# Tree feed-forward: leaves gathered by row from a DRAM table, dotted on VectorE and summed by TensorE through diagonals

## Chip, cores and metric

One core of one Trainium2 chip runs the whole program. The time is device microseconds from start to end of the program on that core; lower is better.

## What is computed

Eight layers follow one another on x, which is 8 x 256 tokens of width 256: each takes a layer norm of x and adds its result to x. The change lies in the second layer, a feed-forward network of 8 binary trees with 255 nodes each:

```python
logits = x @ W_in.T + b_in                      # x is the normed input, W_in is 2040 x 256
decisions = (logits > 0).reshape(B, 8, 255)
acts = silu(logits).reshape(B, 8, 255)
current = 0; dmap = one_hot(current, 255)
for d in range(7):                              # walk from the root to a leaf
    moves = decisions at node current
    current = (current - (2**d - 1)) * 2 + moves + (2**(d + 1) - 1)
    dmap = dmap + one_hot(current, 255)
out = (acts * dmap).reshape(B, 2040) @ W_out.T  # only the 8 nodes on each path count
```

A tree has 127 inner nodes and 128 leaves, and a token ends in exactly one leaf of each tree. The first layer is a cross attention without a softmax, and the third (a masked cross attention with 16 heads) starts when the second has been added to x.

## The kernel before

The five engines have one instruction stream each, written out by hand, with semaphores between them; nothing is planned by a compiler. x stays in SBUF as 16 tiles of 128 tokens. A pair (`i` from 0 to 3) is four such tiles, 512 tokens. Their normed rows `xln` are transposed to `xT` (`transpose_rows` on TensorE, `evacuate_xT` on ScalarE).

The tree stage is a loop over 4 pairs and within each over 8 trees `p`. One turn of it is called a step here. In each step TensorE computes logits with the nodes on the partitions and the tokens along the row: 127 inner nodes (c = 0) and 128 leaves (c = 1), each of two matmuls over the halves of the 256 inputs (L1665). VectorE compares the inner logits with the bias and writes `dec0` (L757). ScalarE computes silu of both banks into `act0` (L1342). One step later TensorE multiplies the decisions with the ancestor matrix `anc` (L1674): for each node the number of right turns minus left turns to it, and where this equals `tgt`, the node is on the token's path. VectorE writes `msk0`, act where it is equal and zero elsewhere (L749). Two steps later TensorE multiplies `msk0` with the output weights `woutT`, for four token tiles and both halves of the nodes (L1687), and sums all 8 trees in PSUM banks 0 and 1. At the end of a pair VectorE adds them to x (`residual`, L666), and the last pair's addition releases the mask load of the third layer (L480).

VectorE also does work of later stages in the stage: layer norm statistics of the next pair (p = 2, followed by `rstd_of` on GpSimd), its rows (p = 3), low bits of weight slices for a later layer (`low_bits`: a mask L670 and a reduction L672 over 1024 each, six slices a pair), sums and ternary rounding of the weights `stage_w1` and `stage_w2` (L698, L712 to L716). SyncE loads the six slices `seen` of the next pair when `Ff.low` says that the last ones were read. ScalarE's queue issues five DRAM to DRAM copies of later weights (L1331) right before the stage, 11 MB in all.

The fp32 matmuls stand in the trace as two records each. GpSimd issues indirect DMAs only in the last layer (`send` L616, the output rows L632).

## Time and profile before

| | |
|---|---|
| median of 3 runs | 1639.69 us (1639.01 to 1641.97) |
| profiled execution, its own time | 1637.88 us |
| its span, first to last instruction | 1636.2 us |
| TensorE busy | 1437.3 us, 88% |
| VectorE busy | 1073.6 us, 66% |
| ScalarE busy | 755.9 us, 46% |
| GpSimd busy | 116.6 us, 7% |
| tree stage, from the page's slices and the chain | 71.5 to 311.2 us |

Busy times of engines overlap, so they don't add up to the span. Engines in the rows: PE is TensorE's matmuls, PEld its weight loads, DVE VectorE, ACT ScalarE, POOL GpSimd, SP SyncE; a q behind a name is the engine's sequencer. A row of the trace gives the start in us, the duration in us, the engine, the line of the program, the operation, what it writes and reads, and in brackets how long the engine sat idle before it and what released it. Of several operations in one row (x8) the duration is that of the group.

### The profile page before, as it was taken

The numbers are of one execution on the slowest core, as the hardware profiler recorded it, in microseconds if no ns is written. First come the engines' busy times: TensorE is split into PE (matmuls) and PEld (weight loads), VectorE is DVE, ScalarE is ACT, GpSimd is POOL, SyncE is SP. The second block draws the span as 40 slices with busy tenths as digits, with TensorE's granted clock in tenths as the row PEclk, the third lists the DMA queues.
The fourth block names the chain that finished last, engine by engine and source line by source line (L and its number), as shares of the span: only waits on it lengthen the run. The fifth ranks groups of instructions, "written<-read, shape, count | busy, mean of one in ns | idle before, by whom it ended". The sixth has DMA issues, their size and how long they took to land.

```text
span 1636.2 us, 26350 instructions
## 1 busy us (share of the span) xinstructions
PE 1437.3 (88%) x9842; PEld 1075.0 (66%) x9849; DVE 1073.6 (66%) x2358; ACT 755.9 (46%) x1264; POOL 116.6 (7%) x168
## 2 busy tenths in 40 slices
PE   7999999878887995799888999999997889999557
PEld 5666666557783443477786878787773677788446
DVE  4455675778877874688856464555548988886344
ACT  2212211257773665476662222222224877788323
POOL 1000000000000000111000000000010011001323
PEclk9999999999998997899989999999998999999779
DMA  9462201320000000000009910000100000000166
GB/s 328 166 201 78 78 2 76 143 68 14 13 3 1 1 1 1 24 14 5 10 2 297 284 28 1 1 1 0 33 7 7 1 7 2 7 28 27 41 183 182
DMA packets 60285, 96.62 MB, mean 59 GB/s; under 512 B 11091, under 2 KB 48972, under 8 KB 59982
## 3 DMA queue, kind: packets, MB, share of 16 engines
q1 hardware_dynamic: 57742, 78.50, 15.0%
q10 hardware_dynamic: 544, 12.16, 2.2%
q0 software_dynamic: 1872, 4.27, 0.7%
q8 instruction: 80, 1.31, 0.3%
q14 instruction: 47, 0.39, 0.1%
HBM read 73.21 MB, written 37.30 MB: 68 GB/s over the span
## 4 chain that ended last, share of the span: by engine, by line
PE 52%; issue 18%; DVE 15%; ACT 6%; DVEq 4%; DMA 2%; SPq 1%; POOL 1%; ACTq 1%; POOLq 1%
PE bank L1995 9%; PE bank L1996 9%; PE bank L1687 7%; PE bank L1665 7%; DVE MB L919 3%; PE bank L1792 3%; DVE plo L937 2%; PE bank L1843 2%; PE bank L1593 1%; PE bank L1796 1%; PE bank L1797 1%; PE bank L1763 1%; DMA jx<-copy_routed 1%; PE bank L1765 1%; PE bank L1725 1%
## 5 line engine op out<-in xcount | busy, mean ns | idle before, releaser
L937 DVE TENSOR_TENSOR plo<-e,phi 120x512 f16<-120x512 f32 x256 | 180.2, 709 | 51.4 <-ACT phi L1417 47.7
L1411 ACT ACTIVATE e<-bank 120x512 f32<-120x512 f32 x256 | 150.6, 588 | 41.0 <-PE bank L1797 31.8
L1417 ACT ACTIVATE phi<-e 120x512 f16<-120x512 f32 x256 | 161.2, 630 | 8.8
L919 DVE TENSOR_REDUCE MB<-bank 128x4 bf16<-128x480 f32 x256 | 155.8, 648 | 13.5 <-PE bank L1765 10.3
L1342 ACT ACTIVATE act<-bank,bin 127x512 f32<-127x512 f32 x64 | 43.1, 687 | 167.2 <-DVE dec L757 163.2
L1665 PE MATMUL bank<-xT,winT 128*127 128x512 f32 (+1 forms) x256 | 114.6, 593 | 1.3 <-ACTq L1313 1.3
L1687 PE MATMUL bank<-woutT,msk 128*128 128x256 f32 (+1 forms) x512 | 115.2, 379 | 0.0
L676 DVE TENSOR_SCALAR high<-raw 128x512 int32<-128x512 int32 x96 | 41.0, 427 | 111.8 <-ACT raw L1546 60.8
L1687 PEld LDWEIGHTS bank<-woutT,msk 128*128 128x128 f32 (+1 forms) x512 | 96.9, 190 | 15.4
L556 POOL TENSOR_TENSOR veps<-mv,ceps 128x4 f32<-128x4 f32 x32 | 8.9, 278 | 1342.6 <-DVEq L647 1210.8
L1995 PE MATMUL bank<-hah,h1w 128*128 128x512 f32 x256 | 101.3, 396 | 3.6 <-DVE hal L679 3.6
L1792 PE MATMUL bank<-Q_even,Kpad_even 128*120 128x256 f16 x512 | 102.1, 282 | 0.5 <-ACT e L1411 0.5
L1792 PE MATMUL bank<-Q_odd,Kpad_odd 128*120 128x256 f16 x512 | 101.4, 280 | 1.1 <-ACT e L1411 1.1
L1996 PE MATMUL bank<-hal,h1w 128*128 128x512 f32 x256 | 100.7, 393 | 0.0
L1995 PE MATMUL bank<-hb,h2w 128*128 128x512 f32 x256 | 100.0, 391 | 0.0
L1996 PE MATMUL bank<-hbl,h2w 128*128 128x512 f32 x256 | 99.7, 389 | 0.0
L1765 PE MATMUL bank<-MB,identb 128*128 128x480 bf16 x256 | 97.8, 382 | 0.0
L1927 PE MATMUL bank<-hpad,taps 128*128 128x512 f32 x192 | 89.2, 601 | 0.9 <-ACT hc L1480 0.9
L1665 PEld LDWEIGHTS bank<-xT,winT 128*127 128x127 f32 (+1 forms) x256 | 48.3, 189 | 51.2 <-issue 49.4
L1792 PEld LDWEIGHTS bank<-Q_even,Kpad_even 128*120 128x120 f16 x512 | 64.5, 138 | 18.5 <-issue 6.8
L1763 PE MATMUL bank<-Kpad_even,Q_even 128*128 128x480 f16 x128 | 51.0, 398 | 28.3 <-DVE Q_even L910 13.3
L1796 PE MATMUL bank<-MBT_even,selm 128*120 128x256 bf16 x256 | 72.2, 282 | 0.0
(308 smaller groups left out, 3520.9 us busy)
## 6 DMA issues: line engine op xcount, KB each, us to landing
copy_routed<-zeros SPq DMA_DIRECT2D x1, 17028.0 KB
jw<-copy_experts SPq DMA_DIRECT2D x23, 385.0 KB, 3.4
seen<-in_h1T SPq DMA_DIRECT2D x8, 512.0 KB, 7.4
seen<-in_h2T SPq DMA_DIRECT2D x8, 512.0 KB, 4.9
h1w<-copy_h1T SPq DMA_DIRECT2D x1, 4096.0 KB, 17.0
h2w<-copy_h2T SPq DMA_DIRECT2D x1, 4096.0 KB, 15.1
ctxp<-in_ctxT SPq DMA_DIRECT2D x13, 240.0 KB, 3.0
jx<-copy_routed SPq DMA_DIRECT2D x23, 132.0 KB, 3.5
```

The source lines that it names most:

```text
L919: dve.tensor_reduce(MB[:, t, h0 // 8, SK + h0 % 8:SK + h0 % 8 + 4], b[:, 0:4 * SK].rearrange("p (h k) -> p h k", h=4), AX.X, ALU.max).then ...
L937: dve.tensor_tensor(plo[:, g % 3, :], e32[:, g % 3, :], phi[:, g % 3, :], ALU.subtract).then_inc(s.lo, 1)
L1411: act.activation(e32[:, g % 3, :], bank[2 + g % 3][0:SK, :], ACT.Exp).then_inc(s.exp, 1)
L1417: act.activation(phi[:, g % 3, :], e32[:, g % 3, :], ACT.Copy).then_inc(s.phi, 1)
L1665: last = pe.matmul(bank[2 + 2 * (p % 2) + c][0:n, :], winT[:, k, w0:w0 + n], xT[:, k, :], start=(k == 0), stop=(k == K2 - 1))
L1687: last = pe.matmul(bank[t // 2][:, (t % 2) * D:(t % 2) * D + D], msk0[0:n, p % 2, c, tok(t)], woutT[0:n, 2 * p + c, :], start=(p == 0 and ...
L1765: pe.matmul(ps, identb[:], MB[:, t, 0, 0:SK].unsqueeze(1).broadcast_to([128, 4, SK]), start=False, stop=True).then_inc(s.ap, 1)
L1792: pe.matmul(ps, K[i % 2][:, v, r, c, b * SK:b * SK + SK], Q[i % 2][:, c, qs], start=(v == 0), stop=False)
L1796: pe.matmul(ps, selm[:], M[i % 2][:, h // 8, qs], start=False, stop=False)
L1927: last = pe.matmul(bank[2 + g % 2][:, :], taps[:, t, j, :], hpad[:, g % 3, :, j:j + S], start=(j == 0), stop=(j == 2))
L1995: pe.matmul(ps, w, hi, start=start, stop=False)
L1996: return pe.matmul(ps, w, lo, start=False, stop=stop)
```

## The change

The leaves' logits and outputs are no longer computed for all 128 leaves. A DRAM table `copy_leaves` of 1024 rows (8 trees x 128 leaves) holds in each row 256 output weights, 256 input weights and the bias, 2052 bytes. The output weights are copied from DRAM to DRAM; the input weights are transposed by TensorE in pairs 2 and 3 of the first layer (16 transposes), copied out by ScalarE and written by one DMA.

In the stage, `g` counts 32 steps over all pairs. TensorE, VectorE and ScalarE keep logits, decisions, silu, mask and output for the 127 inner nodes. Of the leaf counts ScalarE makes a one-hot row (`hot_leaves`), TensorE multiplies it with 0 to 127 (`leaf_number`), VectorE adds the tree's offset and casts (`leaf_numbers`), and GpSimd gathers four times 128 rows (`gather`) into one of three buffers. VectorE multiplies the gathered input weights with the normed rows and sums (`leaf_logits`), ScalarE computes silu of the four columns and three diagonal matrices (`leaf_values`), TensorE adds diagonal times gathered output weights for three tiles (`turned_leaves`), VectorE the fourth (`add_leaves`).

A pair sums in banks 0 and 1 or 4 and 5 in turn, its residual is added at step 5 of the next pair, and the normed rows alternate between `xln` and `xln_odd`. The five weight copies move to steps 3, 9, 14, 19 and 24 of ScalarE's stream. `low_bits` becomes one OR per slice into `seen_low`, with one AND and one reduction at the end. `woutT` holds only inner nodes. Several semaphores are shared with the last layer, whose counts get an offset.

The core of the diff:

```diff
+        def gather(g):
+            pool.wait_ge(Tf.row, g + 1)
+            if g >= GB:
+                pool.wait_ge(Tf.added, g - GB + 1)
+                pool.wait_ge(Tf.turned, g - GB + 1)
+            for t in range(TT):
+                pool.indirect_dma_start(rowsG[g % GB][:, t, 0:ROW], None, leaves[:],
+                                        bass.IndirectOffsetOnAxis(idx[:, g % TREES, t:t + 1], 0),
+                                        bounds_check=TREES * LEAVES - 1, oob_is_err=False).then_inc(st_job[g % GB], 16)
+        for g in range(STEPS):
+            gather(g)
+            if g % TREES == 0:
+                rstd_of(g // TREES + (4 * 1 + 2))
...
         def low_bits(i, q):
-            dve.tensor_scalar(seen_low[:], seen[:, q, :].bitcast(I32), 0xFFF, None, ALU.bitwise_and)
-            dve.drain()
-            dve.tensor_reduce(lowmax[:, ds(i * SEEN + q, 1)], seen_low[:], AX.X, ALU.max)
+            dve.tensor_tensor(seen_low[:], seen_low[:], seen[:, q, :].bitcast(I32), ALU.bitwise_or)
...
+        def leaf_logits(g):
+            rows_in = (xln, xln_odd)[g // TREES % 2]
+            dve.wait_ge(st_job[g % GB], got(g))
+            for t in range(TT):
+                if t == 2:
+                    dve.drain()
+                last = dve.scalar_tensor_tensor(out=dots[:, t % 2, :], in0=rows_in[:, t, :], scalar=1.0,
+                                                in1=rowsG[g % GB][:, t, D:2 * D], op0=ALU.mult, op1=ALU.mult,
+                                                accum_out=lv[:, g % GB, t:t + 1])
+            dve.drain().then_inc(Tf.dot, 1)
+        def add_leaves(g):
+            dve.wait_ge(Tf.val, g + 1)
+            for t in range(len(TURNED), TT):
+                xs = x[:, TT * (g // TREES) + t, :]
+                last = dve.scalar_tensor_tensor(out=xs, in0=rowsG[g % GB][:, t, 0:D], scalar=val[:, g % GB, t:t + 1],
+                                                in1=xs, op0=ALU.mult, op1=ALU.add)
+            last.then_inc(Tf.added, 1)
...
+            for g in range(STEPS + LAG + 1):            # VectorE
+                if g < STEPS and (p or not i):
+                    decisions(g)
+                if 1 <= g <= STEPS:
+                    masked(g - 1)
+                if 3 <= g < STEPS + 3:
+                    leaf_logits(g - 3)
+                if 1 <= g <= STEPS:
+                    leaf_numbers(g - 1)
+                if 4 <= g < STEPS + 4:
+                    add_leaves(g - 4)
+                if g < STEPS and not p and i:
+                    decisions(g)
+                if g >= TREES and g % TREES == LAG % TREES:
+                    tree_residual((g - LAG) // TREES - 1)
+                if g < STEPS:
+                    if p == 1:
                         norm_stats(1, i)
...
+        def leaf_values(g):
+            act.wait_ge(Tf.dot, g + 1)
+            for t in range(TT):
+                last = act.activation(val[:, g % GB, t:t + 1], lv[:, g % GB, t:t + 1], ACT.Silu,
+                                      bias=rowsG[g % GB][:, t, 2 * D:ROW])
+            act.drain()
+            for n, t in enumerate(TURNED):
+                last = act.activation(dgl[:, g % 2, n, :], ident[:], ACT.Copy, scale=val[:, g % GB, t:t + 1])
+            last.then_inc(Tf.val, 1)
...
+            for g in range(STEPS + 3):                  # ScalarE
+                if g in (3, 9, 14, 19, 24):
+                    w, copy = copies[(3, 9, 14, 19, 24).index(g)]
+                    act.dma_start(copy, a[w]).then_inc(w_copied, 16)
+                if i and not p:
+                    evacuate_xT(i + (4 * 1 + 1), 2)
+                if g < STEPS and (p or not i):
+                    inner_values(g)
+                if 1 <= g <= STEPS:
+                    hot_leaves(g - 1)
+                if g < STEPS and not p and i:
+                    inner_values(g)
+                if g >= 3:
+                    leaf_values(g - 3)
...
+            def turned_leaves(g):
+                pe.wait_ge(Tf.val, g + 1)
+                for n, t in enumerate(TURNED):
+                    last = pe.matmul(bank[SUMS[i % 2] + t // 2][:, (t % 2) * D:(t % 2) * D + D], dgl[:, g % 2, n, :],
+                                     rowsG[g % GB][:, t, 0:D], start=False, stop=(p == TREES - 1), skip_group_check=True)
+                last.then_inc(Tf.turned, 1)
+            for g in range(STEPS + 4):                  # TensorE
+                if g < STEPS and (p or not i):
+                    tree_logits(g)
+                if i and not p:
+                    pe.wait_ge(Bf.act, g)
+                    transpose_rows(i + (4 + 1), 2, (xln, xln_odd)[i % 2])
+                if 1 <= g <= STEPS:
+                    right_turns(g - 1)
+                if 2 <= g < STEPS + 2:
+                    inner_outputs(g - 2)
+                if 1 <= g <= STEPS:
+                    leaf_number(g - 1)
+                if 4 <= g < STEPS + 4:
+                    turned_leaves(g - 4)
+                if g < STEPS and not p and i:
+                    tree_logits(g)
```

## Rows read from the trace of the kernel before

**Rows 1.** Busy us of PE, PEld, DVE, ACT, POOL; clock, DMA share, GB/s: tree stage

```profile
71.50:311.20 239.70, 238.33 (x866) 156.71 (x866) 143.46 (x211) 47.41 (x72) 4.83 (x8) 1.00 0.25 88
```

**Rows 2.** Chain that ended last, in order of time, 300 to 330 us

```profile
302.06 0.88 PE bank L1593 x8
302.94 6.93 PE bank L1687 x32
...
309.89 0.69 DVE x L666
...
311.23 2.74 DMA m<-in_mask
```

**Rows 3.** Timeline of one step of the tree stage, 264 to 272 us

```profile
264.85 3.60 PE L1665 MATMUL bank<-xT,winT 128*127 128x512 f32 x8
...
266.76 0.75 DVE L757 TENSOR_SCALAR dec<-bank,negb 127x512 bf16<-127x512 f32 x1 [1.80 <-PE bank L1665]
...
267.60 0.69 ACT L1342 ACTIVATE act<-bank,bin 127x512 f32<-127x512 f32 x1 [5.75 <-DVE dec L757]
...
268.28 0.60 PE L1674 MATMUL bank<-dec,anc 127*127 127x512 bf16 x2
...
268.71 3.62 PE L1687 MATMUL bank<-woutT,msk 127*128 127x256 f32 x16
268.92 1.41 DVE L749 SCALAR_TENSOR_TENSOR msk<-bank,tgt,act 127x512 f32<-127x512 f32 x2 [1.40 <-PE bank L1674]
270.24 1.38 DVE L652 TENSOR_SCALAR xln<-x,mv,rstd 128x256 f32<-128x256 f32 x4
```

**Rows 4.** VectorE's groups by form: busy us, mean ns | idle before

```profile
L672 DVE TENSOR_REDUCE lowmax<-seen_low 128x1 f32<-128x1024 int32 x24 | 29.3, 1220 | 1.8
...
L1272 DVE SCALAR_TENSOR_TENSOR jres<-jw,jx 128x256 f32<-128x256 f32 x23 | 11.0, 479 | 0.0
...
L990 DVE TENSOR_TENSOR x<-x,o 128x1024 f32<-128x1024 f32 x4 | 4.9, 1225 | 0.4
...
L698 DVE TENSOR_REDUCE stage_sum<-stage_w 128x1 f32<-128x2048 f32 x2 | 4.6, 2276 | 0.0
...
L712 DVE TENSOR_SCALAR stage_w<-stage_w,stage_ws 128x2048 f32<-128x2048 f32 x2 | 2.6, 1277 | 0.0
```

**Rows 5.** ScalarE: one group by form, and two operations back to back

```profile
L1568 ACT ACTIVATE jh<-bank,jw 128x128 f32<-128x128 f32 x46 | 14.4, 364 | 19.6 <-PE bank L2095 19.6
...
276.59 1.27 ACT L1342 ACTIVATE act<-bank,bin 127x512 f32<-127x512 f32 x2 [7.42 <-DVE dec L757]
```

**Rows 6.** Indirect DMAs on GpSimd in the last layer; landing is of L632

```profile
1524.94 1.46 POOL L616 DMA_INDIRECT copy_routed<-cells,placei  x1 [0.30 <-issue]
1526.70 0.98 POOL L616 DMA_INDIRECT copy_routed<-cells,placei  x1 [0.30 <-issue]
...
1593.10 0.48 DVE L1284 SCALAR_TENSOR_TENSOR jout<-bank,jx,jres 128x256 f32<-128x256 f32 x1 [0.47 <-PE bank L2104]
...
1594.38 0.97 POOL L632 DMA_INDIRECT out<-jout,jtok  x1 [1.00 <-DVE jout L1284]
...
DMA to landing us min/median/max: 2.0/4.1/5.1
```

**Rows 7.** TensorE by form: small matmuls with a full weight load

```profile
L1823 PE MATMUL bank<-V_even,phi 120*128 120x18 f16 x256 | 21.0, 172 | 6.9 <-DVE plo L937 6.9
```

**Rows 8.** DMA issues: engine, KB each where known, us to landing

```profile
stage_w<-in_w1T SPq DMA_DIRECT2D x1, 1024.0 KB, 10.6
...
f<-copy_f1T SPq DMA_DIRECT2D x1, 1024.0 KB, 5.3
...
copy_h1T<-in_h1T ACTq DMA_DIRECT2D x1, 20.1
copy_h2T<-in_h2T ACTq DMA_DIRECT2D x1, 32.9
```

**Rows 9.** DMA queue of ScalarE's issues: packets, MB, share of 16 engines

```profile
q10 hardware_dynamic: 544, 12.16, 2.2%
```

286 lines of the change are left out of this document (180 added, 106 removed).

## The prediction

> **What bounds the kernel now.** I first read the busy shares by stretch, then the chain of waits, then one step of the tree stage in order of time. Between 71.5 and 311.2 us TensorE is busy 238.3 of 239.7 us at a granted clock of 1.00; VectorE is busy 143.5 us, ScalarE 47.4 and GpSimd 4.8 [rows 1]. The chain says the same: inside the stage it consists of matmuls, with two VectorE residual additions behind the last one, and then the mask load of the next stage takes over at 311.23 [rows 2]. So the stage is bound by TensorE, and whatever leaves TensorE shortens it until something else is late. The reader should see in one step [rows 3] what TensorE does in 7.32 us: eight half matmuls of logits from 264.85 (0.43 us apart, 3.43), two bf16 count matmuls (0.43), sixteen half matmuls of outputs from 268.71 (0.215 apart, 3.44). An fp32 matmul stands in the trace as two records, hence "halves". 32 steps of 7.32 and three turnovers make the 239.7.
>
> **TensorE per step after.** Logits of the 127 inner nodes only: 4 x 0.43 = 1.72. Counts: 0.43 as before. Inner outputs: 8 x 0.215 = 1.72. Diagonal times gathered rows for three tiles: 3 x 2 x 0.215 = 1.29. The four one-column matmuls of the leaf number are not in the trace; the nearest are 18-column matmuls with a 128-column load, 21.0 us busy for 256, so at most 0.08 each [rows 7]; zero from below. I take 0.1 to 0.3 for all four. Sum 5.3 us, against 7.32. If TensorE stayed the bound, 32 x 2.0 = 64 us would go.
>
> **The new wait inside TensorE's queue.** leaf_number(g-1) waits for hot_leaves(g-1), which ScalarE does only after inner_values(g), which waits for decisions(g), which waits for this step's logits. From the step's first matmul: logits to 1.72, the VectorE decision starts 0.2 later and takes 0.75, ScalarE starts 0.09 later [rows 3]; two such ScalarE operations back to back take 0.58 + 0.69 [rows 5]; about 0.1 to TensorE. That is 1.72 + 0.2 + 0.75 + 0.09 + 0.58 + 0.69 + 0.1 = 4.13. TensorE has only counts and inner outputs to do meanwhile and is ready at 3.87. It waits 0.26, then 0.3 for the leaf number and 1.29 for the diagonals: **5.75 us a step**. Queued behind that wait are the diagonals and the next step's logits. This chain has no slack: if VectorE starts a decision late, the step is longer by as much.
>
> **VectorE per step.** Decision 0.75 and mask 0.67 [rows 3]. Four dot products over 128x256 with two fp32 SBUF operands: the nearest row is the scalar_tensor_tensor of L1272, 0.48 us alone [rows 4], about 0.40 apart when back to back (two 512-wide ones take 1.41 together for 0.75 each [rows 3]); with two drains 1.9. No row has its accumulator output; from below it may cost nothing, from above it could double the dots, 1.05 more. I take nothing, since L1272 is the same instruction otherwise. Leaf numbers 0.15, add_leaves 0.45. VectorE starts at 1.92 of a step and is done at 5.85; the next decision is wanted at 5.75 + 1.92 = 7.67, so 1.8 us are free. What the other work needs beyond 1.8 lengthens its step: statistics (about 2.0, by estimate from eight operations the size of tree_rows' and smaller) 0.2; tree_rows 1.4 [rows 3] and the first OR over 1024 (1.23 in the nearest row, L990 [rows 4]), 2.75 with drains: 0.95; residual and OR 2.8: 1.0; magnitudes 2.28 with an OR, twice: 1.8 each; ternary three times 1.28 with an OR, twice: 3.3 each [rows 4]. Three pairs of 2.15, 3.6 and 6.6 make **16.7 us** that TensorE hid before. The OR replaces a mask and a reduction per slice, which is why the one-OR steps fit.
> The Trainium skill ("Vector Engine (DVE) Microarchitecture Reference", Points that are easy to get wrong) says that this shape of instruction with two non-bf16 SBUF sources runs at half throughput, for want of a port to read the accumulator back. L1272 has two such sources without an accumulator and is not slower than its twin that reads PSUM (0.48 us in rows 6), so the trace doesn't show it; with the accumulator it would be the 1.05 us a step above.
>
> **GpSimd and the gathers.** Each step adds four indirect DMAs. Such an instruction takes 0.97 us with 0.30 before the next; one took 1.46. The first starts 0.8 us after its releaser, and one lands 2.0 to 5.1 us after its start, median 4.1 [rows 6]. So a gather of four tiles occupies GpSimd 0.8 + 4 x 1.28 - 0.3 = 5.6 us. It waits for the leaf number (5.4 into the step), for add_leaves and for the diagonals of three steps earlier, which read the same buffer and end at 5.92. From there 0.8 + 3.84 + 4.1 = 8.7: landed at 14.65, wanted by leaf_logits two steps on at 11.5 + 3.3 = 14.8. It fits by 0.15, and VectorE's free 1.8 covers a later landing. The loop through leaf_logits, leaf_numbers and the gather takes 10.95 us for two steps, 5.5 each. I cost it at nothing beyond 5.75, but three chains lie within 5% of each other. rstd_of, moved behind the first gather of each pair, adds two operations to GpSimd's queue (1.2 us of the 4.83 a pair [rows 1], 1.6 with a drain); it is needed two steps later, and the gather behind it can be 1.4 late, which VectorE's free time covers.
>
> **Start, turnovers and end.** In the stage before, 16 leaf transposes (eight took 0.88 [rows 2]) add about 1.05 us with the hand-over to TensorE in each of pairs 2 and 3: the stage starts at 73.6 instead of 71.5. The table's 1 MB goes to DRAM after that; the nearest rows for 1 MB are a quiet load of 5.3 us and one among others of 10.6 [rows 8]; I take 8, landing at 83 (ScalarE issues it near 74.7). The first gather then lands at 83.3 + 3.84 + 4.1 = 91.2, which is 17.6 after the stage's start. Without diagonals steps 2, 3 and 4 could start at 6.05, 10.35 and 14.65, and decision 4 would come at 16.6; but VectorE first owes dots (to 19.5), numbers, tree_rows and an OR, to 22.5. So step 4 is 5.9 late and step 5 starts at 14.65 + 5.75 + 5.9 = 26.3. At each of three turnovers TensorE first transposes (0.95), the xT copies put hot_leaves off until 3.0, the diagonals end at 4.75 and the logits come last, to 6.45; in the next step ScalarE, with leaf_values behind the late logits, is 0.6 late: 1.3 more than a plain step, 3.9 in all. After step 31 nothing hides the last leaf's path: leaf number 5.3, 0.8 and 3.84 of GpSimd, 4.1 to land, dots 1.9, values and three diagonals 1.75 (four small ScalarE operations and three of 128x128, 0.36 alone [rows 5]), matmuls 1.5, residual with drains 1.5, and 0.8 of hand-overs: 21.5 us. The final AND and reduction over 1024 replace one over 24: the reduction takes 1.22 [rows 4], the AND no more, and VectorE's next real work waits for the mask load of 2.74 [rows 2] after two clears; between 0 and 2.4 I take 1.25.
>
> **The weight copies.** They moved from before the stage into it, at steps 3, 9, 14, 19 and 24. The two of 4 MB take 12.8 us each (32.9 - 20.1 [rows 8]), those of 1 MB about 3, a quarter, together 35 of DMA time. No row has a gather beside them. From below nothing (4 MB in 12.8 makes 0.8 us for the 0.26 MB of one indirect DMA, so half the DMA time is free); from above each copy holds a gather for its own length less 2 us of slack, 27. I take 4, near the lower end, by the row of the 1 MB load among others: it took twice its quiet time, shared and not stopped; doubling a transfer of 0.8 us for each of five copies is 4.
> The Trainium skill ("DMA: Bandwidth & Descriptors", Queues, rings and completion order) says that an engine goes round its queues packet by packet. The copies' queue shows few and large packets, 12.16 MB in 544 [rows 9]; taken literally each gather packet would wait for one of those, which gives the upper end. No run here shows it yet.
>
> **Sum.** 73.6 + 26.3 + 27 x 5.75 (155.3) + 3.9 + 16.7 + 4 + 21.5 + 1.25 = 302.6, against 311.2: **8.6 us less**. The profiled execution took 1637.9 us (span 1636.2), so 1629.3; the median of the runs lies 1.8 above it: **1631 us**. The rest of the kernel is unchanged.
>
> **Rivals.**
> *Quicker.* Gathers land in 2.7 us as the mask load does [rows 2], the table in 5.3, and copies cost nothing: 1.4 at the end, 1.4 + 2.7 at the start, 4; about 1621. Speaks for it: loads into SBUF are the short landings here.
> *The saving is eaten.* 0.25 us more a step on the decision chain (hand-overs are estimates) is 27 x 0.25 = 7 us: 1638, no change to be measured.
> *Slower by the copies.* They hold the gathers: +23, 1654. The sign turns when the copies cost 12.6 us in total, 8.6 more than I took. For it: VectorE stands still in leaf_logits when a gather is late, and nothing catches up afterwards. Against: half the DMA time is free.
> *Slower by the dots.* 1.05 more per step: VectorE's free time is 0.75, every extra grows by it, some 16 times, 17 us: 1648.
> *Slower by GpSimd.* At 1.46 + 0.30 each [rows 6] four take 7.04 a step, 225 us for 32 steps; 83.3 + 225 + 6 for rstd_of + 9 for the last leaf's path + 1.25 closes the stage at 325: 1653. The sign turns at 1.65 us apart; only one row reaches it.
> *The change isn't what it says* (rows gathered, but TensorE no less busy) has no support: the removed matmuls are in the diff.
>
> **How the numbers follow.** Forecast 0.36, quicker 0.17, eaten 0.13, copies 0.14, dots 0.12, GpSimd 0.08. A measurement of this kernel tells 0.2% (3.3 us) from no change. Faster: 0.36 and 0.17 less a few hundredths, 0.51; within 0.2%: 0.16; slower 0.33. The range leaves out the edges of the quickest and slowest cases: 1618 to 1655; the forecast's own range is 1625 to 1637.
>
> **What would show it.** Right: a step of 5.75 us with TensorE waiting about 0.3 us before the one-column matmuls; longer steps where VectorE has extras; some 20 us of idle TensorE before the last residual. Wrong: VectorE waiting on DMA in the dots (gathers), above all behind steps 9, 14, 19, 24 (copies); dots over 0.5 us apart; indirect DMAs over 1.4 us apart; steps near 5.3 us.

## The result, and the profile after

The changed kernel takes 1676.1 us (median of 4 runs, 1673.7 to 1683.2), the kernel before 1640.8 beside it: ratio 1.0224, 95% interval 1.0205 to 1.0243. It is 35 us slower, where 9 us less was forecast. The profiled execution took 1683.2 us (span 1681.5), the slowest of the four, so the trace lies 7 us above the median.

The next stage's mask load, which closed the stage at 311.2 us [rows 2], is issued at 344.0. The stretch of [rows 1], for the kernel after (columns: us, then busy time of PE, PEld, DVE, ACT and POOL, granted clock, DMA share, GB/s), and three short pieces of it:

```profile
75.00:344.00 269.00, 204.59 (x802) 133.38 (x802) 171.67 (x476) 103.29 (x297) 144.69 (x136) 0.89 0.65 208
...
137.00:142.00 5.00, 2.36 (x7) 0.96 (x6) 0.24 (x1) 0.00 (x0) 0.00 (x0) 1.00 1.02 420
142.00:147.00 5.00, 3.18 (x8) 2.40 (x9) 4.52 (x20) 1.86 (x8) 1.81 (x2) 0.60 0.80 296
...
235.00:240.00 5.00, 1.80 (x5) 1.27 (x6) 3.59 (x12) 1.84 (x7) 0.73 (x1) 0.52 0.46 181
```

TensorE lost its work as planned, 34 us of busy time although part of what is left ran at half clock, but the stage is 29 us longer than in [rows 1]. From 137 to 142 us VectorE, ScalarE and GpSimd stand still while the DMA engines are full; behind such a hole the granted clock is 0.60, and 0.52 in the last of the pieces, so TensorE is there mostly or all the time at the lower of its two levels, 1.2 GHz. It was 1.00 all through the stage before.

One step, timeline of after; it answers to [rows 3]:

```profile
152.21 0.60 PE L1830 MATMUL bank<-dec,anc 127*127 127x512 bf16 x2
...
153.07 0.74 DVE L807 SCALAR_TENSOR_TENSOR msk<-bank,tgt,act 127x512 f32<-127x512 f32 x1
...
153.73 0.41 DVE L822 SCALAR_TENSOR_TENSOR dots<-xln_odd,rows 128x256 f32<-128x256 f32 x1
...
154.07 0.08 DVE L822 DVE_READ_ACCUMULATOR dots<-xln_odd,rows 128x1 f32 x1
154.07 0.42 DVE L822 SCALAR_TENSOR_TENSOR dots<-xln_odd,rows 128x256 f32<-128x256 f32 x1
...
154.56 0.17 PEld L1837 LDWEIGHTS bank<-leafn,hot 128*128 128x128 bf16 x4 [0.43 <-ACT hot L1467]
154.56 0.25 PE L1837 MATMUL bank<-leafn,hot 128*128 128x1 bf16 x4
...
154.68 1.54 PE L1854 MATMUL bank<-rows,dgl 128*128 128x256 f32 x6
...
157.77 0.60 PE L1830 MATMUL bank<-dec,anc 127*127 127x512 bf16 x2
```

The reader should see a step of 157.77 - 152.21 = 5.56 us: this is what the change was to bring, and when nothing is late it does. The dots are 0.35 apart.

The chain of waits of after (start, us, what) shows what is late instead. In [rows 2] it consisted of matmuls; now most of its longest pieces inside the stage are gathers on their way, of which five are shown:

```profile
118.30 4.21 DMA rows<-copy_leaves,idx
...
130.00 11.73 DMA rows<-copy_leaves,idx
...
179.56 12.36 DMA rows<-copy_leaves,idx
...
199.38 8.59 DMA rows<-copy_leaves,idx
...
225.75 10.36 DMA rows<-copy_leaves,idx
```

And the waits between 60 and 345 us (engine, what waits, for whom: us, times, longest):

```profile
DVE dots L822 <- DMA rows<-copy_leaves,idx: 54.3, 16, 8.9
...
POOL rows L624 <- DVE x L833: 31.3, 7, 8.5
...
POOL rows L624 <- DMA copy_leaves<-table: 21.6, 1, 21.6
...
POOL rstd L602 <- issue: 16.6, 4, 5.0
```

VectorE waits for gathers 16 times, 54 us in all. Four times GpSimd stands 3.8 to 5.0 us in `rstd_of` ahead of its power, which is the drain there.

The indirect DMAs by line (duration, then landing; against [rows 6]):

```profile
L624 POOL DMA_INDIRECT rows<-copy_leaves,idx x128: 993/1007/1797, 83.5 to 332.1; - x128
...
DMA to landing us min/median/max: 3.4/3.9/13.8
```

The median landing is 3.9 us, near the 4.1 of the forecast; it is the maximum, 13.8, that the sum had no room for.

### The profile page after: what moved, and what is told of

The parts are those of the page before. It is cut to its first block, busy times and chain, and to the rows that moved or that the text cites. A ratio compares the mean times of both kernels' runs of the same rounds, so it can differ in the third digit from the quotient of the medians.

```text
span 1681.5 us, 27159 instructions
## 1 busy us (share of the span) xinstructions
PE 1415.0 (84%) x9794; PEld 1059.4 (63%) x9801; DVE 1102.8 (66%) x2625; ACT 814.0 (48%) x1493; POOL 255.9 (15%) x297
## 3 DMA queue, kind: packets, MB, share of 16 engines
q10 hardware_dynamic: 1584, 13.21, 2.3%
## 4 chain that ended last, share of the span: by engine, by line
PE 39%; issue 21%; DVE 16%; DMA 7%; ACT 5%; DVEq 4%; POOL 3%; SPq 1%; POOLq 1%; ACTq 1%
PE bank L2182 9%; PE bank L2183 8%; DMA rows<-copy_leaves,idx 5%; DVE MB L1033 3%; PE bank L1979 3%; DVE plo L1051 2%; PE bank L2030 2%; POOL rows L624 1%; PE bank L1984 1%; PE bank L1983 1%; PE bank L1746 1%; PE bank L1950 1%; DVE dots L822 1%; PE bank L1854 1%; DMA jx<-copy_routed 1%
## 5 line engine op out<-in xcount | busy, mean ns | idle before, releaser
L1033 DVE TENSOR_REDUCE MB<-bank 128x4 bf16<-128x480 f32 x256 | 155.7, 646 | 13.8 <-PE bank L1952 10.4
L624 POOL DMA_INDIRECT rows<-copy_leaves,idx x128 | 139.3, 1088 | 109.9 <-issue 42.3
L1983 PE MATMUL bank<-MBT_odd,selm 128*120 128x256 bf16 x256 | 71.9, 281 | 0.0
L1984 PE MATMUL bank<-MBT_odd,sels 128*120 128x256 bf16 x256 | 71.9, 281 | 0.0
L1984 PE MATMUL bank<-MBT_even,sels 128*120 128x256 bf16 x256 | 70.7, 276 | 0.0
L1979 PEld LDWEIGHTS bank<-Q_odd,Kpad_odd 128*120 128x120 f16 x512 | 61.3, 137 | 10.6 <-issue 3.4
```

Of the source, the lines that this page charges most:

```text
L624: pool.indirect_dma_start(rowsG[g % GB][:, t, 0:ROW], None, leaves[:], bass.IndirectOffsetOnAxis(idx[:, g % TREES, t:t + 1], 0), bounds_ch ...
L1033: dve.tensor_reduce(MB[:, t, h0 // 8, SK + h0 % 8:SK + h0 % 8 + 4], b[:, 0:4 * SK].rearrange("p (h k) -> p h k", h=4), AX.X, ALU.max).then ...
L1979: pe.matmul(ps, K[i % 2][:, v, r, c, b * SK:b * SK + SK], Q[i % 2][:, c, qs], start=(v == 0), stop=False)
L1983: pe.matmul(ps, selm[:], M[i % 2][:, h // 8, qs], start=False, stop=False)
L1984: last = pe.matmul(ps, sels[:, h % 8, :], M[i % 2][:, h // 8, qs], start=False, stop=True)
```

## The experiments

The table gives every run: ratio to the kernel before, median, the stage's end in the profiled execution (issue of the next stage's mask load) and what this execution took from there on. The kernel before: 311.2 and 1326.7; after: 344.0 and 1339.2. The runs came in sets on different chips (e1 to e4, e6 to e13, e14 to e17, e18 and e19), each beside the kernel before on the same chip, so sets are compared by their ratios.

| run | what differs from the changed kernel | median us | ratio (95%) | stage end | rest |
|---|---|---|---|---|---|
| e1_copies_early | copies where they were | 1673.0 | 1.0191 (1.0166-1.0216) | 338.4 | 1340.7 |
| e2_copies_small | copies in halves | 1673.8 | 1.0210 (1.0179-1.0242) | 332.4 | 1336.9 |
| e3_no_drain | no drain in `rstd_of` | 1668.5 | 1.0166 (1.0141-1.0190) | 334.5 | 1335.5 |
| e4_early_nodrain_noseen | e1, e3, no slices | 1646.9 | 1.0038 (1.0023-1.0053) | 310.3 | 1335.5 |
| e6_copies_late | copies at step 31 | 1691.9 | 1.0294 (1.0272-1.0317) | 354.6 | 1340.2 |
| e7_no_seen | no slices | 1679.0 | 1.0226 (1.0209-1.0244) | 340.4 | 1338.9 |
| e8_quiet | e3, e6, e7 | 1667.6 | 1.0163 (1.0136-1.0191) | 325.8 | 1334.7 |
| e9_quiet_numbers_first | e8, numbers ahead of dots | 1684.0 | 1.0261 (1.0236-1.0285) | 347.3 | 1337.8 |
| e10_quiet_base | e3, e7, copies in the next stage | 1635.6 | 0.9972 (0.9961-0.9982) | 300.6 | 1336.7 |
| e11_quiet_add_first | e10, add_leaves ahead of dots | 1638.0 | 0.9983 (0.9964-1.0002) | 299.4 | 1337.9 |
| e12_whole_burst | e11 with all slices | 1648.2 | 1.0061 (1.0043-1.0079) | 308.2 | 1335.8 |
| e13_whole_paced | e12, slices one by one | 1636.2 | 0.9970 (0.9955-0.9985) | 296.1 | 1338.6 |
| e14_drain_behind_gathers | e13, one drain at the end | 1643.4 | 1.0013 (0.9995-1.0032) | 306.8 | 1340.5 |
| e15_warm_tail | e14, nine idle matmuls | 1642.6 | 1.0013 (0.9992-1.0033) | 304.0 | 1338.4 |
| e16_copies_moved | copies in the next stage alone | 1670.2 | 1.0175 (1.0158-1.0191) | 325.7 | 1344.5 |
| e17_before_copies_moved | the kernel before, copies moved | 1641.8 | 1.0008 (0.9996-1.0019) | 313.1 | 1330.6 |
| e18_paced_again | e13 again | 1637.3 | 0.9977 (0.9965-0.9989) | 298.0 | 1339.6 |
| e19_paced_warm | e13, nine idle matmuls | 1635.2 | 0.9972 (0.9958-0.9987) | 298.2 | 1336.9 |

### One cause at a time

The first theory was the prediction's own rival, copies that hold the gathers; beside it stood the drain and the 512 KB weight slices that SyncE loads six at a time.

e1_copies_early, the copies back in the first layer:

```diff
                 evacuate_xT(i + 2)
+                if i == 1:
+                    for w, copy in w_in.items():
+                        act.dma_start(copy, a[w]).then_inc(w_copied, 16)
```

> The changed kernel (1676 us) with the five DRAM to DRAM weight copies issued in the first layer, after the second pair's xT copies, so that none of the 11 MB runs beside a gather. Theory C, the copies hold the gathers: the waits of 7.2, 5.7 and 7 to 11 us in the dots behind steps 9, 14, 19 and 24 go, together some 25 us: about 1651. Theory D, the drain in GpSimd's rstd_of waits for the gathers in flight: nothing changes, 1670 to 1676. Theory P, the pipeline of three buffers is itself too slow: at most 8 us go.

1673.0. The 25 us of theory C did not come, because the copies had only met another victim: the table's landing grew from 7.3 to 17.2 us and the first gather started at 95.0 instead of 83.5. From there the stage was 17 us quicker than the changed kernel's.

e2_copies_small, each copy as two DMAs of half the columns:

```diff
-                    act.dma_start(copy, a[w]).then_inc(w_copied, 16)
+                    for c in range(0, copy.shape[1], copy.shape[1] // 2):
+                        act.dma_start(copy[:, c:c + copy.shape[1] // 2],
+                                      a[w][:, c:c + copy.shape[1] // 2]).then_inc(w_copied, 16)
```

> The changed kernel with each weight copy issued at the same place as two DMAs over half the columns, so that its runs are 2 KB (512 bytes for the last one) instead of long contiguous ones. If the copies hold a gather because their packets are large, gathers get their turn and 10 to 20 us go: 1656 to 1666. If the copies only share bandwidth, or do nothing, 1676, or some us more because short runs move more slowly.

1673.8, no difference that the intervals can tell. The traces do tell one. The page of the changed kernel has 13.21 MB in 1584 packets on ScalarE's queue, that of e2 the same 13.21 MB in 8656, and the gathers that met a copy were used 3 to 4 us sooner: that of step 12 8.6 us after its last issue instead of 12.4, that of step 17 7.4 instead of 10.4. The DMA queues of e2 from 178 to 190 us (packets, MB, share of the 16 engines' time; q10 carries the copy, q0 the gathers):

```profile
q10 hardware_dynamic: 1122, 2.26, 56.7%
q0 software_dynamic: 621, 2.05, 45.6%
```

With packets of 2 KB copy and gather share the engines about evenly by bytes. But the copy lasts longer for it, 23.3 us to the landing of the second half of `copy_h1T` instead of 16.4 for the whole, so more gathers meet it. e2's profiled execution ended its stage 12 us earlier, but it is e2's fastest and that of the changed kernel is its slowest; what the small packets are worth in total stays open.

e3_no_drain, GpSimd's addition done by VectorE, so that no drain is needed:

```diff
             pool.wait_ge(ln_var, n)
+            if 6 <= n <= 9:
+                pool.tensor_tensor(rstd[:], veps[:], mhalf[:], ALU.pow).then_inc(ln_rstd, 1)
+                return
```

> The changed kernel with the variance plus epsilon of the tree stage computed on VectorE, so that GpSimd does the power alone and needs no drain between the first and the second gather of a pair. Theory D: the 5.0 + 3.9 + 3.8 + 3.9 us that GpSimd stood in the drain go from its queue; each puts off a gather that has little slack, so 10 to 16 us go: about 1663. Theories C and P: 0 to 4 us.

1668.5, by the ratios 9.5 us less. The drain sits behind the first gather of a pair and waits for the gathers in flight. In pairs 2 to 4 the gather behind it starts 5.8 to 6.5 us after its leaf number, without the drain 1.4 to 1.7.

e7_no_seen, slices of 16 columns for pairs 2 to 4:

```diff
-                sp.dma_start(seen[:, q, :], slices[SEEN * i + q]).then_inc(ld_h1, 16)
+                n = HID if i == 0 else 16
+                sp.dma_start(seen[:, q, 0:n], slices[SEEN * i + q][:, 0:n]).then_inc(ld_h1, 16)
```

> Left out: the six 512 KB weight slices that SyncE loads for each of pairs 2 to 4 are cut to 16 columns; all instructions stay, the OR over the slices runs over old data. Theory 'transfers': the bursts of six slices (3 MB) hold the gathers of steps 6, 14 and 22 (VectorE waits of 7.2, part of 3.4, and 4.3 us, plus the second gather behind each), so 12 to 15 us less, about 1663. Rival: only the copies and the drain matter, 1673 to 1676.

1679.0: nothing. The trace says why. With the slices gone the steps fell otherwise against the copies, and the gathers of steps 12 and 16 met them: VectorE waited 7.1 and 13.6 us. The last indirect DMA of step 16 started at 204.85 us, the 4 MB copy at 205.58 (timeline of e7):

```profile
205.58 0.50 ACTq L1488 DMA_DIRECT2D copy_h2T<-in_h2T  x1
...
222.17 0.43 DVE L823 SCALAR_TENSOR_TENSOR dots<-xln,rows 128x256 f32<-128x256 f32 x1 [13.61 <-DMA rows<-copy_leaves,idx]
```

VectorE used the gather 17 us after its last issue instead of 4.

e16_copies_moved, SyncE issues copies and their loads behind the next stage's mask loads:

```diff
+            if L is L1X:
+                for w, copy in w_in.items():
+                    sp.dma_start(copy, a[w]).then_inc(w_copied, 16)
+                sp.wait_ge(w_copied, W_COPIED)
...
```

> The changed kernel with one thing undone: the five copies and the loads that depend on them are issued by SyncE behind the next stage's mask loads, nothing in the tree stage. Drain, bursts and VectorE's order stay. It is the price of the copies by themselves; the run with the copies at the last step reached the decision of step 28 at 275.0 us instead of 290.9 before its copies began. Theory 'transfers': stage end 344 - 16 = 328, total about 1660. Rival (early and small copies brought 2 to 3 us): 1673.

1670.2: 8 us less by the ratios. In the profiled executions the stage is 18 us shorter, but those two don't lie alike to their medians.

### All together

e4_early_nodrain_noseen: e1, e3 and e7 in one.

> Copies early as in the first kernel of this set, no drain as in the third, and of the weight slices loaded into seen in pairs 2 to 4 only 16 of 1024 columns (the rest of the low bits of those slices is left out). So the gathers have the DMA engines to themselves. If the copies, the drain and these loads together are the cause, the time comes down to what the sum of the prediction gave without them, 1627 to 1635. If the pipeline itself is slower than its sum (Theory P), it stays above 1645, with steps above 6.5 us where nothing but gathers is in flight.

1646.9, by the ratios 30 us less than the changed kernel, where e1, e3 and e7 by themselves gave 5, 9.5 and nothing. Much of what is left is the late table: its first gather starts at 96.0.

e6_copies_late and e8_quiet put the copies at the last step instead:

```diff
+                if g == STEPS - 1:
+                    for w, copy in w_in.items():
+                        act.dma_start(copy, a[w]).then_inc(w_copied, 16)
```

> The five weight copies (12 MB) are issued by ScalarE at the last step of the tree stage instead of at steps 3 to 24; nothing else differs from the changed kernel, and the table is written at its own time, which the run with early copies did not allow (there its landing grew from 7.3 to 17.2 us). Theory 'transfers': gathers behind the copies land late and the time is not made up; in the changed kernel VectorE waited 5.7, 3.4 and 8.9 us in the dots of steps 12, 14 and 17 behind the two 4 MB copies, so the stage should end 15 to 20 us earlier (mask load issued near 326 instead of 344.0) and the total be about 1659. Rival 'copies cost nothing' (the early copies brought 3 us, the small ones 2): mask load at 341 to 344, total 1673 to 1676. The copies now run into the next stage's loads, which can cost it a few us; the mask load's time is the reading that decides.

> The changed kernel without GpSimd's drain in rstd_of (the addition on VectorE), copies at the last step, slices of pairs 2 to 4 cut to 16 columns (left out): the gathers run alone. Against the run with early copies only the table's landing differs (about 7 instead of 18 us after its issue). If that start counts whole, 12 us less than its 1646.9: 1635, stage end near 304. If the start is hidden by something else, 1645 to 1647. What is left above a 5.6 us step is then neither copies, slices nor drain: theory 'loop' expects steps of 6.0 to 6.3 us, set by the two-step loop gather start -> dots 8.0, dots 1.6, leaf numbers, 1.4 to the next gather but one: 12.1 for two steps; theory 'decision chain' expects 5.6.

Both missed in the total, for one reason, and it became the clearest measurement of the contention. ScalarE reaches step 31 while the gathers of steps 28 to 31 are still to land. Timeline of e8:

```profile
258.79 1.00 POOL L628 DMA_INDIRECT rows<-copy_leaves,idx  x1 [0.30 <-issue]
...
264.70 0.59 ACTq L1492 DMA_DIRECT2D copy_f1T<-in_f1T  x1
...
267.80 0.68 ACTq L1492 DMA_DIRECT2D copy_f3T<-in_f3T  x1
...
284.93 0.43 DVE L829 SCALAR_TENSOR_TENSOR dots<-xln_odd,rows 128x256 f32<-128x256 f32 x1 [14.10 <-DMA rows<-copy_leaves,idx]
306.74 0.43 DVE L829 SCALAR_TENSOR_TENSOR dots<-xln_odd,rows 128x256 f32<-128x256 f32 x1 [15.93 <-DMA rows<-copy_leaves,idx]
```

11 MB of copies are issued from 264.7 on; the gather of step 28, whose last issue was at 264.5, is used 20 us after it, and that of step 29 comes at 306.7, 35 us after its last issue. That is as long as the copies take (34.8 us from issue to landing for the last of them in the kernel before). The DMA queues of e8 from 274 to 282 us, where the engines wait for that gather, show how:

```profile
q10 hardware_dynamic: 32, 2.10, 79.1%
q0 software_dynamic: 32, 0.13, 8.7%
```

The engines take one packet of the copy and one of the gather in turn, but a packet of the copy has 66 KB and one of the gather 4 KB. So the gather of step 29 came out only with the copies' end, and in e2, with packets of 2 KB, it did not have to. Up to there both traces answered the question. The decision of step 28 is at 290.9 us in the changed kernel, 275.0 in e6 and 248.4 in e8.

e10_quiet_base has the copies in the next stage, no drain, no slices:

> As the quiet kernel (no drain in rstd_of; slices of pairs 2 to 4 cut to 16 columns, which is left out), but the five copies and the loads that follow them are issued by SyncE behind the mask loads of the next stage, so that nothing but gathers is on the DMA queues in the tree stage. The quiet kernel reached the decision of step 28 at 248.4 us (before any copy), the one with early copies at 262.8 and ended its stage 47.5 us later, at 310.3 (mask load). Theory 'transfers': the end comes at 248.4 + 47.5 = 296, 14 to 15 us earlier than in the kernel before (311.2); total 1646.9 - 14.3 = 1633. Rival: copies and loads in the next stage cost what they cost here, 1640 or more, with the mask load at 296 all the same.

1635.6. The mask load comes at 300.6 where 296 was expected: the decision of step 28 is 3.2 us later than in e8, of which 1.6 are there at the first decision and 1.1 come by step 5, and the tail took 1.5 more. This kernel shows the change with nothing but gathers beside it (and slices left out that the kernel before loads), and it is quicker than the kernel before: 10.6 us in the stage, 4.6 in total.

### What sets a quiet step

e9_quiet_numbers_first and then e11_quiet_add_first change VectorE's order only (the moved lines go from their old place):

```diff
+                if 1 <= g <= STEPS and g != 2 * TREES:
+                    leaf_numbers(g - 1)
                 if 3 <= g < STEPS + 3:
                     leaf_logits(g - 3)
```

```diff
+                if 4 <= g < STEPS + 4:
+                    add_leaves(g - 4)
                 if 3 <= g < STEPS + 3:
                     leaf_logits(g - 3)
```

> As the quiet kernel, and VectorE writes the leaf numbers of step g-1 before the dots of step g-3 instead of behind them (step 16 excepted), so that the next gather no longer waits for the dots of the one two before. Theory 'loop': the two-step loop of 12.1 us was the bound of quiet steps; without it steps fall to 5.6 to 5.75 (hot chain, diagonals), 0.4 x 27 = 11 us less than the quiet kernel, or about 5 where VectorE's extra work takes over part of it: 1624 to 1630. Theory 'decision chain': no change, within 2 us of the quiet kernel.

> As the quiet base, and VectorE's add_leaves(g-4) stands ahead of the dots of step g-3 instead of behind leaf_numbers(g-1). In the quiet steps the gather starts 1.37 us or more behind the leaf numbers, and behind add_leaves, which takes 0.45 to 0.5 of it; with the numbers first it was 3.14 each time, so add_leaves is the releaser. Theory 'loop through the dots' (12.1 us for two steps): the loop falls by 2 x 0.45, up to 0.45 x 27 = 12 us, of which the 5.56 us decision chain leaves some 4 to 8; total about 1627. Theory 'decision chain': nothing, 1633.

Both expectations of the "loop" theory fell. With the numbers first the steps got longer: from decision 8 to decision 24 it is 116.5 us, 103.4 in e8. VectorE now stands before the leaf number with nothing to do, the dots come behind it, add_leaves behind them, and the gather starts 3.14 us after its number in nearly every step. With add_leaves first the gather starts up to 0.7 us earlier in its step (1.1 once), in some steps no earlier, and nothing changes: 103.9 us in e11, 104.2 in e10, for 16 steps. A step of plain work is 5.56 in both. So the gather wasn't seen on the path there; what exceeds 5.56 are VectorE's extras and the turnovers.

### Slices, and a version that is quicker than both

> Nothing left out: no drain, copies and their loads behind the next stage's mask loads, add_leaves first, and the six slices of a pair loaded in one burst as in the changed kernel. Against the one before it in this set only the three bursts come back: each makes two gathers 4 to 5 us late (5 to 9 us of stage time by the run with copies late, where VectorE waited 4.6, 3.4 and 4.0 us). Theory 'transfers': 12 to 18 us more, 1641. Rival: three bursts vanish in VectorE's free time, 1627 to 1630.

> As the one before, but a slice of 512 KB is loaded as soon as VectorE has finished with its slot, one per step in steps 3 to 7 of a pair, instead of six at once at the pair's end. The bytes are the same. Theory 'a late gather costs what exceeds its slack': a single slice holds a gather by about 1.3 us (3 MB took 8 to 9), 18 slices at most 18 us less what is hidden: 3 to 8 us above the kernel without slices, 1632, and under the kernel before (1641). Rival 'bytes count, not bursts': same as with bursts, within 3 us.

e13 frees a slot as soon as it is read:

```diff
             for q in range(SEEN):
+                if i >= 1:
+                    sp.wait_ge(Ff.low, SEEN * (i - 1) + q + 1)
                 sp.dma_start(seen[:, q, :], slices[SEEN * i + q]).then_inc(ld_h1, 16)
```

For that VectorE signals `Ff.low` with each OR, and its drain at the end of a pair goes. The same bytes in bursts cost 12.8 us by the ratios (e12 against e11), one by one nothing that can be told (e13 against e11). Windows of e12 and e13, the whole stage up to the mask load:

```profile
75.00:308.00 233.00, 191.65 (x800) 125.56 (x798) 171.75 (x480) 102.95 (x296) 144.95 (x132) 0.94 0.63 190
...
75.00:296.00 221.00, 187.69 (x802) 124.15 (x801) 171.63 (x480) 103.01 (x296) 146.25 (x132) 0.96 0.66 200
```

Both move 44 MB in the stage (GB/s times us), e13 in 12 us less and with a higher DMA share. So for the slices it was not the amount of traffic. The changed kernel moves 56 MB there; the difference is the copies. e13 leaves nothing out and moves the copies as e16 does; it takes 1636.2 us, 0.3% less than the kernel before. Measured a second time (e18) it is 0.23% less, interval 0.11 to 0.35.

> The whole kernel with paced slices, unchanged, with more rounds. It was 0.3% faster than the kernel before (1636.2 us); the same kernel with one more drain behind the last gather, in idle time, was 1643.4, and its profiled run lost 5 us in one turnover where the granted clock halved (a set of diagonals 2.91 us instead of 1.54, logits 3.81 instead of 1.88). Theory 'the clock falls in some executions and not in others, in the waits that the change leaves TensorE': the times spread over 10 us or more and the median lies at 1636 to 1643. Rival 'the drain cost the 7 us': 1636 again, with a spread like that of the kernel before.

> The kernel before the change with the same move of copies and loads, to see whether the move is worth something by itself, and so against what the whole kernel with paced slices has to be held. In the kernel before TensorE is busy through the copies (71 to 106 us) and nothing waits for them: theory 'no cost where TensorE binds': within 1 us of the kernel before. Rival 'the 6 MB of loads beside the first mask loads cost the next stage': 2 to 4 us less.

e18's times lie between 1631.7 and 1639.1 us, within a smaller spread than those of the kernel before beside it (1636.7 to 1646.5), so the theory of a clock that falls in some executions and not in others found no support. e17 shows that moving the copies is no gain by itself (1.0008). The credit belongs to the change with its transfers put in order. The kernel before was not run with paced slices; VectorE and the loads aren't what it waits for [rows 1].

### Where the rest of the gain goes

e13's stage ends 15 us earlier than that of the kernel before, and its total is only 4 to 5 us less. The time from the mask load on, 1326.7 us in the kernel before and 1330.6 in e17, is 1334.7 to 1344.5 in each kernel with gathers. Of the 12.5 us of the changed kernel 4.5 lie between the first and the fifth mask load, 0.3 between the fifth and the sixth, 2.4 between the sixth and the ninth and 5.4 behind it.

> The whole kernel with paced slices, plus one drain of GpSimd's own right behind the last gather, where GpSimd has nothing to do for 38 us. In every kernel with gathers the first drain of the next stage takes 1.8 to 2.4 us longer than in the kernel before (the power behind it starts 2.4 to 3.3 us behind the variance sum instead of 1.0), and the ScalarE normalisation and the keys behind it come as much later. Theory 'the first drain behind gathers has work of its own to do, whenever it comes': the 1.8 us move into idle time, stage-to-stage time falls by 1.8 us, total 1634 to 1634.5. Rival 'any drain after a pause of the same length is slow': nothing changes, 1636.

One part is shown by GpSimd's first `rstd_of` of the next stage, in the kernel before, after, and e14:

```profile
337.22 0.66 POOL L560 TENSOR_SCALAR nmean<-mv 128x4 f32<-128x4 f32 x1
338.03 1.04 POOL L562 TENSOR_TENSOR rstd<-veps,mhalf 128x4 f32<-128x4 f32 x1
```

```profile
371.24 0.66 POOL L600 TENSOR_SCALAR nmean<-mv 128x4 f32<-128x4 f32 x1
374.34 1.04 POOL L602 TENSOR_TENSOR rstd<-veps,mhalf 128x4 f32<-128x4 f32 x1 [2.44 <-issue]
```

```profile
334.47 0.66 POOL L606 TENSOR_SCALAR nmean<-mv 128x4 f32<-128x4 f32 x1
335.27 1.04 POOL L608 TENSOR_TENSOR rstd<-veps,mhalf 128x4 f32<-128x4 f32 x1
```

From the start of `nmean` to that of `rstd` it is 0.81 us before, 3.10 after and 0.80 in e14; over all kernels with gathers and without the added drain the first drain takes 1.4 to 2.3 us more, although in the changed kernel the last gather landed 35 us earlier, and the normalisation and the keys wait for it. With a drain in idle time it is gone, and the stretch from the first to the fifth mask load is 113.7 us (e14) and 112.7 (e15) against 115.0, 116.6 and 115.7 (e13, e18, e19); it was 111.6 before, and 113.0 in e17, which has the copies there too.

> As the one before, and TensorE does nine matmuls of 128x512 whose result nobody reads (4, 2 and 3 of them) in the waits for the last gathers (4.2, 2.0 and about 2 us idle in the last 15 us of the stage). There the granted clock is 0.74 and then 0.50, the last two sets of diagonals take 2.93 us instead of 1.54, and the next stage's first 7 us run at 0.79 where the kernel before had 1.00. Theory 'the idle tail costs clock': sets of 1.54 again, stage end 2 to 3 us earlier and 1 to 2 us in the next stage, 3 to 4 less in total than the kernel with the drain alone. Rival 'the clock there is not on the path, or the extra matmuls delay the real ones': within 1 us, or slower.

> The same kernel with the nine matmuls in TensorE's waits of the last 15 us and without the added drain: the tail's clock alone. Theory 'clock in the tail': 2 to 4 us less than the run beside it. Rival 'it does not reach the total': within 1 us of it.

```diff
                 if 4 <= g < STEPS + 4:
                     turned_leaves(g - 4)
+                for n in range({STEPS + 1: 4, STEPS + 2: 2, STEPS + 3: 3}.get(g, 0)):
+                    pe.matmul(bank[2][:, :], woutT[0:INNER, 0, 0:128], msk0[0:INNER, 1, :], start=True, stop=True)
```

The clock does what was expected. The last stretch of e13 and the entry of its next stage, then the same of e15:

```profile
282.00:296.00 14.00, 6.43 (x15) 3.87 (x13) 5.37 (x20) 3.67 (x14) 2.64 (x3) 0.62 0.28 80
296.00:303.00 7.00, 5.88 (x20) 4.15 (x20) 6.15 (x14) 2.94 (x8) 0.00 (x0) 0.79 0.25 59
```

```profile
289.00:304.00 15.00, 11.95 (x38) 6.66 (x37) 5.88 (x21) 4.45 (x17) 4.24 (x5) 1.00 0.34 101
304.00:311.00 7.00, 5.40 (x23) 3.33 (x21) 6.17 (x13) 3.51 (x8) 0.00 (x0) 1.00 0.26 62
```

With matmuls in the waits the clock stays at 2.4 GHz; from decision 31 to the mask load it is 26.1 us (e15) instead of 27.9 (e14), and 24.6 (e19) instead of 27.8 (e18); the stretch to the fifth mask load is about 1 us shorter in both. In the total this is 0 (e15 against e14) to 2 us (e19 against e18), both within the intervals. The totals of e14 and e15, some 7 us above e13 by the ratios, say nothing on drain or clock: their traces have pauses on several engines that name neither an instruction nor a DMA, five in each stage, of 0.9 to 5.8 us, and e13, e18 and e19 have none. One of them in e14:

```profile
125.32 0.60 ACT L1433 ACTIVATE xT<-bank 128x512 f32<-128x512 f32 x1 [1.98 <-remote]
...
126.04 0.75 DVE L817 SCALAR_TENSOR_TENSOR msk<-bank,tgt,act 127x512 f32<-127x512 f32 x1 [1.75 <-remote]
...
127.43 2.91 PE L1858 MATMUL bank<-rows,dgl 128*128 128x256 f32 x6
```

The diagonals behind the pause take 2.91 us instead of 1.54, the half clock again. Whether the added drain, the kernel's place in memory or the chip causes the pauses was not settled; e16 and e17 ran on the same chip and have none in the stage.

Some 8 to 10 of after's 12.5 us stay open. Stretches with the same instructions differ from kernel to kernel: the fifth to the sixth mask load takes 234 to 238 us, the last stretch of the kernel, 169.4 us before, 168 to 170 or 172 to 180, and among the kernels with gathers there are some at either end of each. In that last stretch (1466.8 us to the end before, 1507.4 after) the mean granted clock is 0.86 in the kernel before and 0.83 after, 174.1 us long, so the clock is lower where the time is longer; whether it is the cause, and why it falls for longer in one kernel than in the other, was not found.

## Why the prediction was wrong

*What bounds the kernel.* Right: TensorE. Its work left, and something else was late.

*Step and TensorE's new wait.* Right: 5.75 forecast (its own terms, 4.13, 0.3 and 1.29, make 5.72), 5.56 measured. The wait for the one-hot row stands where it was put: 0.43 us for the weight load of the leaf number, and for the matmul about 0.2 where 0.26 was forecast.

*VectorE.* Right, a little dear: four dots take 1.6 us instead of 1.9. The accumulator has a record of its own:

```profile
L822 DVE SCALAR_TENSOR_TENSOR dots<-xln,rows 128x256 f32<-128x256 f32 x64 | 24.7, 424 | 31.4 <-DMA rows<-copy_leaves,idx 29.7 <-issue 0.4
...
L822 DVE DVE_READ_ACCUMULATOR dots<-xln,rows 128x1 f32 x64 | 5.3, 82 | 0.0
```

0.42 us and 0.08, mostly overlapped. The rival "slower by the dots" is out. So is the rule of the Trainium skill ("Vector Engine (DVE) Microarchitecture Reference", Points that are easy to get wrong) by which this shape with two fp32 SBUF sources runs at half throughput: by that it would be the 1.05 us more a step of that rival.

*Start, extras, turnovers, tail.* Right as a sum. Without the 4 us for copies it ended the stage at 298.6 us; e10, where nothing but gathers was left on the queues, ended it at 300.6. Step 5 started at 103.9 (its decision at 105.8 less the 1.92 of [rows 3]) and not at 99.9; the 27 steps with their extras took 172.9 us and not 175.9; the tail 23.8 and not 22.75. So the start was 4.0 us too early and the steps 3.0 too long; that these nearly cancel is luck.

*GpSimd.* Pace right (1.30 us apart in most cases; the rival with 1.76 is out), start too quick: 1.2 to 1.4 us after its releaser instead of 0.8. But the drain was priced at 0.4 and called covered. It waits for the gathers in flight, 3.8 to 5.0 us in each pair. The prediction named the queue that `rstd_of` was moved into and did not ask what a drain does in it.

*What stands beside a gather: the step that failed.* Every gather was priced at the median landing of 4.1 us, the copies beside it at 4 us in all, the drain at nothing, as covered by VectorE's free time, and SyncE's bursts of six slices not at all. Together they cost 43 us of stage (344.0 - 300.6) and 41 in total. The experiments price them in two ways. Taken alone out of the changed kernel, copies, bursts and drain gave 8, 0 and 9.5 us. Put back one after the other onto e11, bursts cost 13 us (e12 against e11), the drain 19 (e16 against e12, which also differ in VectorE's order, under 2 us by e10 and e11) and the copies 8 (the changed kernel against e16). So the size of one depends on which others are there; e7 shows it, where without the bursts the gathers of steps 12 and 16 met the copies instead. In both ways the copies are the smaller part, inside the prediction's 4 to 27 (by its own rule, 35 less 2 for each of five, the end is 25), and drain and bursts, which stood in the sum at nothing, the larger.

The reason for the 4 us was that half the DMA time is free and that a 1 MB load among others had been shared, not stopped [rows 8]. Shared is right for packets of like size: beside a burst of slices a gather landed 8 to 9 us after its last issue instead of 3.9 (12 where a copy of 1 MB came too). The copies' packets are large: the gather of step 29 waited 35 us for the end of 11 MB of copies in e8, that of step 16 in e7 17 us for the end of one of 4 MB. The Trainium skill ("DMA: Bandwidth & Descriptors", Queues, rings and completion order) has an engine go round its queues packet by packet, and the traces agree: 32 packets of the gather between 32 of the copies in e8. The prediction took it for the pessimistic end, from [rows 9], and it is what happens to a gather that meets a copy; the copies' cost in total, 8 us, still lay nearer the lower end.

SyncE's bursts were there before as well, with median landings of 4.9 to 7.4 us, and nobody waited for them; now these are 9.3 to 10.4 and the last of a burst takes 12 to 18, and each burst held two gathers.

*The sign's turning point.* The prediction let the copies' rival decide from 12.6 us on. The copies alone, 8 us in total, would not clearly have turned the sign; with drain and bursts, 41, it was far on the other side.

*The rest of the kernel is unchanged.* Wrong by 12.5 us in the profiled execution. 2.3 are the first drain, about 1 the clock that an idle tail leaves behind; the rest is open, as above.

The 53.9 us between forecast and profiled execution (1683.2 - 1629.3) are so 41.4 in the stage (344.0 - 302.6) and 12.5 behind it (1339.2 - 1326.7).

## What to carry to other kernels

A transfer that engines wait for has to be priced at its worst landing, not its median: list everything that any queue issues while it is under way, also what was harmless before, with its packet size, and pace it, since the same bytes one slice at a time cost nothing here and in bursts 13 us. The price of one such cause depends on the others, so undo them together before judging any one alone, and put them back one by one. And look where an idle engine leaves its clock, and what a drain has to wait for, before calling the rest unchanged.

## What the runs showed of the hardware

- An indirect DMA of 128 rows of 2052 bytes occupies GpSimd for 1.0 us, the next starts 1.3 us after it, and it lands 3.9 us (median) after its own start, at most 5.3 in e4, where copies, drain and bursts are gone. Beside large transfers the last of four landed up to 12.4 us after its start in the changed kernel and 35 us in e8.
- Two queues with work took turns packet by packet: in 8 us of e8 32 packets of a copy (2.10 MB) and 32 of gathers (0.13 MB); in 12 us of e2, with copy packets of 2 KB, 2.26 MB of copy and 2.05 MB of gathers.
- GpSimd's drain behind indirect DMAs in flight took 3.8 to 5.0 us, and the first one after 128 of them still 1.4 to 2.3 us more than without gathers, 2.3 of them in the changed kernel, where the last had landed 35 us before. Behind an earlier drain in idle time (e14, e15) the surplus was gone.
- TensorE's granted clock was 1.00 while it was busy all the time. In the tail it fell to 0.5 (1.2 GHz) in e13 during a wait of 4.2 us and stayed there behind the next, of 2.0 us; in e15 matmuls whose result nobody reads filled most of these waits, and it stayed at 1.00, also behind a wait of 2.1 us.
